# One block for three stages: ternary feed forward, normed attention and routing laid side by side, slot by slot

## The reference: what is computed

```
x = x + L0_ffn(layernorm(x))      # "f0": bit_linear (ternary weights, 8-bit activations) 256->1024,
                                  #   depthwise conv of width 3, silu, bit_linear 1024->256
x = x + L1_xattn(layernorm(x), ctx)   # "a1": sim = q k^T, sim normalised over its whole (q, k) plane,
                                  #   softmax over keys, times v, times Wo
x = x + L1_ffn(layernorm(x))      # "r": logits = relu(x rw1 + rb1) rw2 + rb2, top 2 of 8 experts,
                                  #   position of each choice in its expert (cap 1024); then "e": the experts
```

## Time and profile before

| | us |
|---|---|
| median of 3 runs | 4931.16 |
| lowest, highest run | 4923.28, 4934.56 |
| span of the profiled execution | 4930.8 |
| last `y_out` of f0 ends / first DVE work of a1 | 1042.45 / 1054.85 |
| a1's DVE at its slot 6 (first `score_spread`) | 1067.80 |
| last `y_out` of a1 ends / first DVE work of r | 1214.64 / 1227.07 |
| r's first `up` matmul / `up` of its second batch | 1232.28 / about 1242.3 |

### The profile page before, as it was taken

One profiled execution on the slowest core, in us unless ns is written; L12 is line 12 of the kernel. 1 busy time (PEld: TensorE's weight loads), 2 busy tenths in 40 slices (PEclk: granted clock), 3 DMA queues, 4 the chain that ended last, 5 costly groups with the idle time before them and its releaser, 6 DMA issues. The chain is left out here.

```text
span 4930.8 us, 90627 instructions
## 1 busy us (share of the span) xinstructions
PE 4484.1 (91%) x31852; PEld 3484.2 (71%) x31852; DVE 3190.3 (65%) x9752; ACT 2002.6 (41%) x4154; POOL 1819.8 (37%) x2248
## 2 busy tenths in 40 slices
PE   7999769988995999789996999999999977999979
PEld 5666547767884888667774788888888644777856
DVE  6888689967553332178883788888888843444344
ACT  3555357744442322145552334434334332222234
POOL 2222146532454332155540233333333303666533
PEclk9999889988997999899997999999999989999989
DMA  4666512235223222122222011001110083222233
GB/s 116 155 149 153 125 57 70 63 114 168 61 57 74 71 71 69 54 72 68 76 59 74 27 34 28 28 28 29 30 34 24 17 258 106 88 88 87 72 113 105
DMA packets 332892, 391.32 MB, mean 79 GB/s; under 512 B 66485, under 2 KB 301466, under 8 KB 321690
## 3 DMA queue, kind: packets, MB, share of 16 engines
q1 hardware_dynamic: 319130, 360.28, 25.9%
q0 software_dynamic: 13312, 25.25, 2.2%
HBM read 296.33 MB, written 89.10 MB: 78 GB/s over the span
## 5 line engine op out<-in xcount | busy, mean ns | idle before, releaser
L2549 PE MATMUL fa_h<-fa_xnT,fa_w 128*128 128x256 f32 x2048 | 485.4, 383 | 0.0
L2561 PE MATMUL fa_y<-fa_w,fa_hT 128*128 128x256 f32 x2048 | 462.5, 379 | 0.0
L2549 PEld LDWEIGHTS fa_h<-fa_xnT,fa_w 128*128 128x128 f32 x2048 | 380.5, 191 | 81.9 <-issue 27.5
L2561 PEld LDWEIGHTS fa_y<-fa_w,fa_hT 128*128 128x128 f32 x2048 | 386.9, 190 | 65.0 <-issue 15.4
L2424 ACT ACTIVATE fa_hT<-fa_h,fa_b 128x256 f32<-128x256 f32 x512 | 214.6, 470 | 534.5 <-PE fa_h L2549 473.1
L425 DVE TENSOR_REDUCE a_mx<-a_score 128x16 f32<-128x1920 f32 x128 | 276.1, 2157 | 53.4 <-PE a_score L609 53.3
L2942 ACT ACTIVATE m_hT<-m_h,m_b 128x256 f32<-128x256 f32 x256 | 107.4, 470 | 363.2 <-PE m_h L3003 363.2
L1566 PE MATMUL r_h<-r_xnT,r_rw 128*128 128x256 f32 x1024 | 247.3, 390 | 0.7 <-ACT r_xnT L1516 0.7
L1867 ACT ACTIVATE e_hT<-e_h,e_b 128x256 f32<-128x256 f32 x256 | 107.3, 470 | 335.0 <-PE e_h L1921 335.0
L1706 POOL DMA_INDIRECT e_xg<-moe_rows,e_idx x64 | 128.6, 2009 | 307.9 <-issue 254.8
L3003 PE MATMUL m_h<-m_hnT,m_w 128*128 128x256 f32 x1024 | 235.7, 379 | 2.5 <-ACT m_hnT L2932 2.5
(11 more groups left out here) (463 smaller groups left out, 10820.2 us busy)
## 6 DMA issues: line engine op xcount, KB each, us to landing
a_floor<-a_lowest SPq DMA_DIRECT2D x64, 960.0 KB, 8.6
cv_toep<-kernels SPq DMA_DIRECT2D x16, 2048.0 KB, 9.5
x<-a_xo SPq DMA_DIRECT2D x96, 256.0 KB, 4.3
f_xb<-x SPq DMA_DIRECT2D x64, 256.0 KB, 3.0
f_xres<-x SPq DMA_DIRECT2D x64, 256.0 KB, 3.0
a_xb<-x SPq DMA_DIRECT2D x64, 256.0 KB, 3.0
e_w<-in_L_ffn_ew SPq DMA_DIRECT2D x16, 1024.0 KB, 7.6
a_cb<-in_ctx SPq DMA_DIRECT2D x96, 90.0 KB, 2.9
```

Of the source, the lines that this page charges most:

```text
L2549: last = pe.matmul(h_ps[j % 2][:, c, :], w1[:, e, k, f:f + P], xnT[it.p][:, k, :], start=k == 0, stop=k == KD - 1)
L2561: last = pe.matmul(bank[:, t * D:(t + 1) * D], hT[e % 2][:, k, t * P:(t + 1) * P], w2[:, e, k, :], start=k == 0, stop=k == KE - 1)
```

## The change

The three stages become *parts* of one block. A part is a program for each engine plus the slot at which it starts: f0 at 0, a1 at 32, r at 64. In each slot every engine issues f0's steps, then a1's, then r's. So f0's slots 32 to 39 share their turn with a1's slots 0 to 7, and a1's slots 32 to 40 with r's slots 0 to 8. The steps and their order inside a part are the same.

```diff
+    def slot(self, s, n, depth):
+        if s == self.begin:
+            self.start()
+        self.once.get(s, nothing)()
+        for lag, step in self.steps:
+            if 0 <= s - lag < n:
+                step(It(s - lag, s - lag, 0, n, self.unroll))
+        if s == n + depth - 1:
+            self.finish()
...
+def side_by_side(parts, programs):
+
+    begin = min(part.first + program.begin for part, program in zip(parts, programs))
+    end = max(part.first + part.n + part.depth for part in parts)
+    for t in range(begin, end):
+        for part, program in zip(parts, programs):
+            program.slot(t - part.first, part.n, part.depth)
...
+def end_all(nc, stages):
+    for s in dict.fromkeys(s for stage in stages for s in stage.sems):
+        nc.sync.sem_clear(s)
+    nc.all_engine_barrier()
```

SBUF: a1 gets an area of its own (48,640 bytes of each partition), f0 and r share the rest. PSUM: the banks are laid out so that a1's bank k is f0's bank k and r's is a1's, and the first use of a bank waits for the last reader of the part before:

```diff
-    qt_ps, aux, aux2, y_ps = st.ps("qt_ps", [P, KD * S], BF16), st.ps("aux", [P, 512]), st.ps("aux2", [P, 512]), st.ps("y_ps", [P, TL, D])
-    h_ps, c_ps = ([st.ps(f"{n}{p}", [P, 2, S]) for p in two] for n in ("h_ps", "c_ps"))
+    aux = st.ps("aux", [P, 512])
+    h0, h1, c0 = (st.ps(n, [P, 2, S]) for n in ("h_ps0", "h_ps1", "c_ps0"))
+    qt_ps, aux2 = st.ps("qt_ps", [P, KD * S], BF16), st.ps("aux2", [P, 512])
+    c1, y_ps = st.ps("c_ps1", [P, 2, S]), st.ps("y_ps", [P, TL, D])
...
+    t_ps, s0, s1, m_ps, gu_ps, y0, p_ps, y1 = (st.ps(n, [P, 512]) for n in ("t", "s0", "s1", "m", "gu", "y0", "p", "y1"))
...
+            if it.i == 0:
+                pe.wait_ge(*before["hidden"])
...
+            if it.i == 0:
+                pe.wait_ge(*before["conv"])
...
+                if it.i == 0 and m == 1:
+                    pe.wait_ge(before["exps"], 2 * (B - 1))
```

The three shown are a1's first `scores` on f0's last `h_out`, a1's first `sum_moments` on f0's last silu, and r's first `up(1)` on a1's exps of batch 30. Loads wait for the store of the batch that they read:

```diff
         def load(it):
+            sp.wait_ge(before["stored"][it.p], 16 * (it.h + 1))
             if it.reused(4):
                 sp.wait_ge(xn_ready, it.i - 3)
```

```diff
+    f0, f0_after, ternary = ternary_feed_forward(nc, const, x0, x1, wf, 0, Area((mid, SBUF_END)))
+    a1, a1_after, attention = normed_attention(nc, const, x1, x0, ctx, wa, B, Area((at, mid)), f0_after)
...
+    r, routing = route(nc, const, x0, rows, table, meta_at, meta_w, wr, 2 * B, Area((mid, SBUF_END)), a1_after, f0_after)
+    run_parts(nc, [ternary, attention, routing])
+    end_all(nc, [f0, a1, r])
```

More of the change, by code:

```diff
@@ L8 @@
+import math
 from contextlib import ExitStack
@@ L974, in _, with tensor, start @@
+    def tensor(pe):
+        def start():
             for m in two:
@@ L1246, in _, with tensor, fold, once @@
+    def tensor(pe):
+        def fold(n, left, right):
+            def once():
+                if n:
+                    pe.wait_ge(fold_out, n)
+                else:
+                    pe.wait_ge(weights, 64)
+                    pe.wait_ge(*before["turned"])
                 for half in two:
                     for k in range(KD):
-                        last = pe.matmul(bank[half][0:CP, 0:D], left[:, k, half * CP:(half + 1) * CP], right[:, k, :], start=k == 0, stop=k == KD - 1)
+                        last = pe.matmul(gu_ps[0:CP, half * D:(half + 1) * D], left[:, k, half * CP:(half + 1) * CP], right[:, k, :],
+                                         start=k == 0, stop=k == KD - 1)
@@ L1310, in normed_attention, with turn_x @@
-    st.end()
-def route(nc, const, src, xn_all, table, meta_at, meta_w, w):
-    st = Stage(nc, "r", [const["apart"]])
+            return once
+        def turn_x(it):
+            pe.wait_ge(xn_ready, it.i + 1)
+            if it.i == 0:
+                pe.wait_ge(*before["row"])
+            if it.reused(1):
+                pe.wait_ge(xT_ready, it.i)
+            for t in range(TL):
+                for k in range(KD):
+                    last = pe.transpose(t_ps[:, k * S + t * P:k * S + (t + 1) * P], xn[it.p][:, t, k * P:(k + 1) * P],
+                                        const["ident"][:])
+            last.then_inc(x_turned, 1)
@@ new lines, in sum_moments, with turn_p @@
+        def sum_moments(it):
+            pe.wait_ge(moments, MOM * (it.i + 1))
+            if it.i == 0:
+                pe.wait_ge(*before["conv"])
+            if it.reused(1):
+                pe.wait_ge(spread, SPR * (it.i - 1) + 1)
+            pe.matmul(m_ps[:, 0:2], const["ones"][:], mom[it.p][:], start=True, stop=True).then_inc(m_done, 1)
+        def turn_p(it):
+            pe.wait_ge(exp_ready, 2 * it.i + 2)
+            if it.reused(1):
+                pe.wait_ge(pT_ready, it.i)
+            for t in range(TL):
+                last = pe.transpose(p_ps[0:SK, t * P:(t + 1) * P], pr[it.p][:, t, :], const["ident"][:])
+            last.then_inc(p_turned, 1)
@@ new lines, in attend @@
+        def attend(it):
+            pe.wait_ge(pT_ready, it.i + 1)
+            pe.wait_ge(u_ready, it.i + 1)
+            if it.i == 0:
+                pe.wait_ge(*before["row2"])
+            if it.i == 1:
+                pe.wait_ge(*before["y"])
+            if it.reused():
+                pe.wait_ge(y_ready, it.i - 1)
+            for t in range(TL):
+                last = pe.matmul(y_ps[it.p][:, t * D:(t + 1) * D], prT[it.p][:, t, :], u[it.at][:], start=True, stop=True)
+            last.then_inc(y_done, 1)
@@ new lines, in tensor, with route @@
+        return Program([(5, scores), (4, project_context), (8, attend), (3, turn_x), (7, turn_p), (5, sum_moments)], 4,
+                       once={FOLD: fold(0, wk, wq), FOLD + 1: fold(1, wv, wo)})
+    after = dict(turned=(xT_ready, B), context=(u_ready, B), keys=(g_ready, B), exps=exp_ready, spread=(spread, SPR * B), turned_p=(pT_ready, B), stored=stored)
+    return st, after, Part(first, B, DEPTH, sync, gpsimd, vector, scalar, tensor)
+def route(nc, const, src, xn_all, table, meta_at, meta_w, w, first, area, before, room):
+    st = Stage(nc, "r", area=area)
```

1224 lines of the change are left out of this document (625 added, 599 removed).

## The result

The changed kernel took 4895.36 us (median of 4 runs, 4891.48 to 4895.79), the kernel before 4930.0 beside it (4 runs). The ratio is 0.9926, with a 95% interval of 0.9912 to 0.994. I had forecast 4894. A second measurement of both on another chip of the same pace gave 4890.28 against 4932.87, ratio 0.9913 (0.99 to 0.9927).

The account below looks back on a forecast made before the run. Stage ends were taken as bound by one batch's latency chain, then store, clears, barrier and loads. Gains 22.3 + 20.7 − 4.6 − 1.0 = 37.4 us off the 4930.8 span gave 4894 us, range 4884 to 4911.

Parts of the forecast that it names:

- forecast case: Whole kernel: both borders overlap, gaining 33 to 41 us, for 4890 to 4898 us; chance 0.50.
- First border: f0 to a1: `score_spread` directly behind f0's last `y_out` gains 25.35 us, less two terms of 1.5, so 22.3.
- The folds: f0's end on PE: a1's added folds take 1.85 us each; 1.5 us reach f0's chain, the second costs nothing.
- What is held back: f0's end: the last `down` stands behind a1's first `sum_moments` on PE, up to 3.6 us late; 1.5 taken.
- DVE's added work: f0's late slots: a1's `norm_stats` (about 1.0 us) and `norm` (0.73) replace f0's own or lie in waits; zero cost.
- The rule weighed: Both borders: shorter pauses would keep PE's full clock, 3 us more gain; not adopted, the 1.5 us clock terms kept.
- Second border: a1 to r: r's second batch starts at 1220.1 instead of 1242.3, 22.2 us, less 1.5 for clock: 20.7.
- The clears: r's end: 101 semaphore clears instead of 28, a cost of 4.2 to 5.1 us; 4.6 taken.
- r's early loads: During a1: r's weights load among a1's loads, costing between nothing and 4 us; 1 taken.
- That a border doesn't hand over: One border's parts still run behind each other, gain 27 us, or 19 if both (4912); chance 0.06, plus 0.04 near no change.
- That middle slots lengthen: Middle of the three stages: batches 0.49 us longer lose the gain and 10 us; 0.7 gives 4960; chance 0.03.
- PE in order at 1.2 GHz: Both borders: `down` waits for `sum_moments`, r's first batch runs half its time at half clock; gain 26, 4905; chance 0.20.

Follow-up runs that it names:

- norm: Changed kernel with a1's `norm` of batches 0 to 2 moved on DVE behind f0's `hidden_max`; 4922.25 us, ratio 0.9899, where before took 4973.86.
- clears: Changed kernel with the 101 semaphores at the shared end cleared as ranges; 4924.49 us, ratio 0.9898, where before took 4973.86.
- twoin: Changed kernel with a1's `norm` of batches 0 to 2 left in place but written as a two-input `scalar_tensor_tensor`; 4897.02 us, ratio 0.9926.
- both: Changed kernel with a1's `norm` behind `hidden_max`, r's `norm` and `norm_stats` (slots 65 to 68) behind `score_spread`, shared clears as ranges; 4883.84 us, ratio 0.9904.
- best: Changed kernel with a1's and r's DVE steps moved into better places and clears as ranges at every stage's end; 4869.32 us, ratio 0.987.
- b1only: Changed kernel with only f0 and a1 sharing a block, then a barrier and r in its own block; 4912.78 us, ratio 0.9958.
- b2only: Changed kernel with f0 in its own block, then a barrier, and only a1 and r sharing a block; 4913.62 us, ratio 0.9966.
- changed2: Changed kernel unedited, measured a second time on another chip of the same pace; 4890.28 us, ratio 0.9913.
- again: Changed kernel unedited, on a chip of another pace where before took 4973.86; 4924.72 us, ratio 0.9906.
- fill: Changed kernel with r's `norm` and `norm_stats` of slots 65 to 69 moved on DVE behind a1's `score_spread`; 4926.27 us, ratio 0.9903.

## Why the prediction was right, and where it wasn't

The forecast case came true, with 4895.36 for 4894: both borders overlap as forecast, and the size is right. That it is right to 1.4 us is luck: the changed kernel's own two medians lie 5 us apart, and the gain was 34.6 us in the first measurement and 42.6 in the second. The sum was 37.4; the pieces give 23.2 (H, 56.6 against the mean of 80.0 and 79.5), 18.7 (S, 453.8 against 472.5) and −3.5 to −5.0 (C), so 37 to 38. Inside the sum several terms were off and cancelled.

- **First border, forecast 22.3, measured 23.2.** The place was right: `score_spread` right behind f0's last `y_out`. Two of the three corrections were not. *The folds* I put at 1.5. In norm, where only they, a1's projections and DVE steps that nothing shuts out are in f0's way, f0's last `hidden_max` starts 35.5 us behind the fourth last (1019.76 less 984.24) against 33.7 before (1021.49 less 987.77): 1.8. *What is held back*, 1.5, was wrong in sign: `down` of batch 31 started when ACT's copy ended, 1039.74, and ran at full clock, so that from its start to `y_out` it took 2.2 us instead of 4.05 and gave 1.9 back. The hold-up that I had priced exists all the same, where half clock lasts longer: in clears (0.77 in 1027 to 1042) ACT's copy ended at 1040.80, but the last `down` started at 1042.58, behind `sum_moments` at 1042.34, 1.8 us late; in twoin it was 1.2 us, in both 0.9. *DVE's added work*, "zero", was wrong: `norm`, 0.73 us by its row, was shut out beside POOL. That cost 2.3 more at the last `hidden_max` (37.8 us behind the fourth last in the changed kernel). From the start of f0's last `y_out` to `score_spread` 25.4 us went (26.2 before, 0.8 now), and 25.4 − 1.8 − 2.3 + 1.9 = 23.2. Two errors cancelled: 2.3 us that I had at nothing, and 3.4 that I was too low with `down` (1.9 given back where I took 1.5 off). That was luck.
- **The rule weighed.** I kept 1.5 us at each border for a clock that by the Trainium skill's rule, weighed in the prediction, would have stayed up. The last `down` sided with the rule; yet half clock came at 1030 to 1033, behind gaps of 2.13 and 1.61 us, in the changed kernel and not in norm. At the second border the trace sided with me: the granted clock was 0.57 in 1180 to 1184 and again in 1187 to 1191. For the time, my bounds of 0 to 3.6 were on the wrong side of zero, since the old `down` was itself at half clock.
- **Second border, forecast 20.7, measured 18.7** (19.2 against the first profile of before alone). To r's second batch it was as forecast: 153.2 us from `score_spread`, 174.5 before, 21.3. But I let all three leftover `attend` and two `turn_p` stand ahead of the second batch, 3.1 us (3.35 by the prices that I gave). Only one of each does (1194.92 to 1196.00); the others come later, and by r's end 2.1 us of the 21.3 are gone again. In turn the late slots cost more than the 4.5 us that I added: r's first `up` came 5.9 us late by the same count (143.0 us from `score_spread` against 137.1 to the same place before), because on POOL r's root now stands ahead of a1's, and DVE's wait grew from 1.13 to 1.68. r's first 16 matmuls took 5.39 us, 1.7 over full clock, for which I had 1.5.
- **The clears, 4.6, measured 3.5 to 5.0.** Right, and clears and best show that they are on the path.
- **r's early loads, 1, measured 0.** From a1's slot 15 to its slot 32, with r's loads in between, the `score_shift` steps lie 77.4 us apart (1083.66 to 1161.02), 77.6 before (1108.54 to 1186.10). DVE waited for no load from 990 to 1210.
- **The rivals.** That a border doesn't hand over falls with H and S; b1only and b2only show what it looks like. That middle slots lengthen falls: 4.53 us a slot in both. PE in order at 1.2 GHz would have needed half clock over slots 68 and 69; it covered two stretches of under 4 us, the second over most of r's first 16 matmuls.
- **What would show it.** `score_spread`, PE's idle stretches (2.1 us at most) and the clears were as said. f0's last `y_out` was to come at 1044 to 1046 and came at 1041.98; r's second batch was to come 43 us early and came 46.3: 1.6 us of both are the scatter of f0's earlier part; the rest of the first is the balance of the terms above.

## What to carry to other kernels

Where pipelined stages follow each other, the drain of one and the fill of the next are worth more than the barrier between them: here 8.7 us for taking the barriers away, some 35 to 43 for interleaving. When steps of one stage are laid beside those of another, look engine by engine at what runs at that moment, not only at the step's own duration: two vector instructions of 0.7 us together become 5 beside a GpSimd multiply of 4.5 us, and a wait for another engine's result is worth filling with the guest's steps (6.19 to 4.44 us a slot). Clear semaphores as ranges: 101 took 6.2 us, two ranges about 0.2.

## What the hardware showed that I had not expected

- **POOL and DVE.** What counts is each single instruction, and a `norm` has two, the second 0.30 us behind the first. The third `norm` of the changed kernel began 0.36 us ahead of the multiply and still took 5.03 us: its second instruction began 0.06 ahead and took 4.73. In changed2 it began 0.53 ahead and took 0.70. The starts in the trace are not sharp: an instruction that began 0.03 us ahead lost in the changed kernel (1005.85, multiply from 1005.88, 4.53 long) and won in twoin (1005.69, multiply from 1005.72, 4.82 long). POOL loses at most some 0.3 us in this way, DVE up to 4.3, as the one instruction lasts 4.5 us and the other 0.4.
- **Chips differ in some stages.** On the other chip the kernel before took 4973.86 and the changed one 4924.72. H is the same there (56.5), but r's batches took 10.2 us instead of 9.4, and E 3380 to 3389 us instead of 3360 to 3370. In r, ACT starts its copy late. ACT, then PE, of again:

```profile
1407.46 0.58 ACT L1643 COPY r_xnT<-r_t 128x512 f32<-128x512 f32 x1 [2.50 <-remote]
```

```profile
1405.15 0.60 PE L1682 MATMUL r_t<-c_ident,r_xn 128*128 128x128 f32 x4
```

  `turn_x` ends at 1405.75 and ACT starts 1.7 us later. No experiment was made on it, and its cause stays open, as does why the change gained 49 us there (4973.86 less 4924.72) and 35 to 43 elsewhere.
- **The clock at f0's end** was 1.00, 0.89 and 0.77 in 1027 to 1042 in norm, the changed kernel and clears, with nearly the same instructions in it. clears and again have the same program up to there and ran on the same chip, and yet H is 58.2 in clears and 56.5 in again (granted clock 0.89). The same holds for r's first 16 matmuls: 5.38 or 5.39 us in the changed kernel, changed2, b2only, norm and clears, 6.67 in twoin, and 3.70 in again and in the three kernels that fill a1's late slots (fill, both and best). Whether the filling keeps the clock up there is not shown.
